# A separate prologue for two batches in a fused attention and routed feed-forward kernel

## The chip, the cores and the metric

The kernel runs on one core of a Trainium2 chip. The metric is the device time in microseconds; each kernel is run several times and the median is compared. The profile is of one execution.

## What is computed

Eight batches of 256 rows of 256 values pass through one layer: x plus cross attention of its layer norm over a context (16 heads of 16, a strictly lower triangular mask, softmax), and then plus a feed-forward of eight experts of which each row takes two, within a capacity. Cut to what matters:

```python
qh = (layernorm(x) @ W_q).reshape(B, S, 16, 16)
kh = (ctx @ W_k).reshape(B, S, 16, 16)
vh = (ctx @ W_v + b_v).reshape(B, S, 16, 16)
scores = einsum('bihd,bjhd->bhij', qh, kh) / 4
probs  = softmax(where((j < i) | (i == 0) & (j == 0), scores, -inf))
x = x + einsum('bhij,bjhd->bihd', probs, vh).reshape(B, S, 256) @ W_o + b_o
x = x + routed_ffn(layernorm(x), wg, w1, b1, w2, b2)   # top 2 of 8
```

All of it is float32; the kernel splits operands into high and low parts to get there with faster matmuls.

## The kernel before

The program has two parts, attention() and experts(). The change is in attention() alone. There every engine has an order written out by hand: its function defines small pieces (queries, keys, a_scores, exp, maxima, split_queries, mask and so on) and a step(s) that calls them, and steps() runs step(s) for s from -2 to 8. One step works on up to four batches at once: it projects batch s+2 (proj_part), finds the maxima of batch s+1 (max_part), computes the probabilities and the values of batch s (score_part) and writes out batch s-1 (out_part). Engines meet only at semaphores, which each piece waits for and counts up.

For one batch the pieces follow one another so:

- Projection. SyncE loads the context into c_sb and ScalarE rounds it to cT_hi (round_context), GpSimd takes the rest, cT_lo (split_context). VectorE gathers the statistics of x (norm_stats, next_stats), GpSimd makes the scale and shift (powers, norm_powers), ScalarE normalises (norm_x), TensorE transposes (turn_x, line L808), ScalarE rounds to xT_hi (L401), VectorE takes the rest, xT_lo (L566). Then queries and keys (project_turned, twelve matmuls each, L851) go to bank[1] and bank[0] in PSUM. Of each result ScalarE takes q_h or k_h (L401), VectorE the rest (q_rest, k_rest, L574), GpSimd the middle and low parts (split_rest, L263 and L265), and SyncE stacks the parts by DMA into Qs and Ks (stack, L202), three transfers of the high part, two of the middle and one of the low for each.
- Maxima. a_scores computes twelve units of scores (L752) with a mask (L755), VectorE reduces each to its maximum (maxima, L596); a unit may begin when the reduction two units back is done. split_maxima, turn_maxima (L840) and copy_maxima (L472) bring the maxima into two rows of Qs by a DMA on ScalarE's queue (L474).
- Probabilities and values. b_scores (L766, L769) in four groups of four heads, exp (L423), mask on GpSimd (L323 to L325), values (L785, L786), with V from project_values (L862) and add_value_bias (L613).
- Output. turn_values (L801), normalise, turn_attention, outputs, add_output, the second layer norm and the router.

The weights are split once: round_weights on ScalarE (L398), split_weights on VectorE (L561). project_values writes bank[0], which the keys of the same step use too, so it waits for k_rest and, the first times, for all four weights:

```python
            def project_values(s):
                if first(s, 1):
                    pe.wait_ge(k_rest_ready, s + 2)
                    pe.wait_ge(w_lo_ready, 4)
                project(bank[0], 2, cT_hi, cT_lo, v_done)
```

Steps -2 and -1 are the prologue. Step -2 projects batch 0. Step -1 on TensorE is project_values (batch 0), turn_x (batch 1), all twelve units of maxima of batch 0, turn_maxima, and then queries and keys of batch 1. Step 0 is of the general form, with queries and keys of batch 2 in it.

Of the kernel before, what the change touches and what calls it, by code (L numbers as in the profile page):

```python
# [6 lines left out]
P = 128  # L7
# [9 lines left out]
HEADS = 16  # L17
# [26 lines left out]
def attention(nc, sem, sb, persist, x, ctx_in, Wq, Wk, Wv, bv, Wo, bo, wg, w1, b1, w2, b2, xn_rows, out):  # L44
# [20 lines left out]
    bank = [ps[:, 2, :], ps[:, 6, :]]  # L65

# [10 lines left out]
    c_sb = sb("c_sb", [P, 2, S], F32)  # L77
    xn = sb("xn", [P, 2, D], F32)
    st1 = sb("st1", [P, 2, 6], F32)
    mv1 = sb("mv1", [P, 2, 2], F32)  # L80
    ve1 = sb("ve1", [P, 2, 2], F32)
    rs1 = sb("rs1", [P, 2, 2], F32)
# [31 lines left out]
    x0_loaded, x_loaded = sem("x0_loaded"), sem("x_loaded")  # L114
    ctx_loaded = sem("ctx_loaded")
# [33 lines left out]
    def steps(step):  # L149

        for s in range(-2, B + 1):
            step(s)
# [22 lines left out]

    def first(s, n):

        return s < n
# [6 lines left out]
    with block:  # L185

        @block.sync
        def _(sp):
            sp.dma_start(x_all[:, 0:2, :], x_tiles[:, 0:2, :]).then_inc(x0_loaded, 16)
            sp.dma_start(c_sb[:, :, :], ctx_tiles[0]).then_inc(ctx_loaded, 16)  # L190
            sp.dma_start(w_raw[:, 0], Wq.rearrange("(k p) n -> p k n", p=P)).then_inc(wqkvo_loaded[0], 16)
            sp.dma_start(w_raw[:, 1], Wk.rearrange("(k p) n -> p k n", p=P)).then_inc(wqkvo_loaded[1], 16)
            sp.dma_start(w_raw[:, 2], Wv.rearrange("(k p) n -> p k n", p=P)).then_inc(wqkvo_loaded[2], 16)
            sp.dma_start(w_raw[:, 3], Wo.rearrange("(k p) n -> p k n", p=P)).then_inc(wqkvo_loaded[3], 16)
            sp.dma_start(x_all[:, 2:, :], x_tiles[:, 2:, :]).then_inc(x_loaded, 16)
# [9 lines left out]
            def step(s):  # L205
                to = (s + 2) % BUFS
                if proj_part(s) and s + 3 < B:
                    sp.wait_ge(cT_lo_ready, s + 3)
                    sp.dma_start(c_sb[:, :, :], ctx_tiles[s + 3]).then_inc(ctx_loaded, 16)
                if proj_part(s):  # L210
# [11 lines left out]
                    sp.wait_ge(k_h_ready, s + 3)  # L222
                    stack(Ks[to], K_PARTS, "h", k_part["h"], k_stacked)
# [8 lines left out]

            steps(step)
# [4 lines left out]
        def _(pool):  # L238
            pool.dma_start(bv_bc[:, :], bv.rearrange("(a n) -> a n", a=1).broadcast_to([P, D])).then_inc(small_loaded, 16)
            pool.dma_start(bo_bc[:, :], bo.rearrange("(a n) -> a n", a=1).broadcast_to([P, D])).then_inc(small_loaded, 16)  # L240
# [100 lines left out]
            def step(s):  # L341
# [19 lines left out]
                if s == -1:  # L361
                    norm_powers(2)
# [1104 lines left out]
```

## Time and profile before

| | us |
|---|---|
| median of 3 runs | 475.74 (475.26 to 476.03) |
| the profiled execution | 474.79 |
| its span | 473.0 |
| TensorE busy in the span | 378.9 (80%) |
| VectorE busy | 294.4 (62%) |
| GpSimd busy | 227.1 (48%) |
| ScalarE busy | 188.2 (40%) |
| granted TensorE clock, mean | 0.908 |

Attention takes about the first 225 us of the span and the experts the rest. A busy share says how long an engine worked, not what it was waited for; a timeline's row shows the idle time before it in brackets and what ended it. The granted clock is 1.00 at 2.4 GHz and 0.50 at 1.2 GHz.

### The profile page before, as it was taken

To read this page: it belongs to the slowest core of one execution; us is meant where nothing else is said; L and a number is where in the kernel's file an instruction comes from. 1 tells how busy PE (TensorE), PEld (TensorE's weight loads), DVE (VectorE), ACT (ScalarE), POOL (GpSimd) and SP (SyncE) were. 2 spreads that over 40 slices of the span, in tenths; PEclk is the share of its full clock that TensorE was granted. 3 is DMA by queue.
4 is the path that set the end of the run, shared out by engine and by line. 5 is a ranking of instruction groups with operands and counts; after the bars stand their busy time and mean duration, and the time that the engine had idled before them with its cause. 6 is when DMAs were issued, how large, how long until landed. Compare 5 with 4: busy or idle time off the path is not lost. (4 is left out here: it accounts for less than half of the span.)

```text
span 473.0 us, 8086 instructions
## 1 busy us (share of the span) xinstructions
PE 378.9 (80%) x3005; PEld 320.8 (68%) x3026; DVE 294.4 (62%) x614; ACT 188.2 (40%) x255; POOL 227.1 (48%) x311
## 2 busy tenths in 40 slices
PE   0566589999989898976422689999999999999970
PEld 0545467777768686664311479898989898999960
DVE  3445366776777666742269676868676777777540
ACT  3212345655555563634112252526262626262210
POOL 5773964756666662523114840717171717150504
PEclk9858799999999999988555599999999999999995
DMA  7621463606152528122110610818181818140303
GB/s 220 202 67 36 122 178 72 178 28 177 47 158 60 145 54 228 46 92 95 57 39 11 245 56 2 230 49 232 47 239 37 242 37 246 34 52 1 45 1 44
DMA packets 35735, 49.10 MB, mean 104 GB/s; under 512 B 4734, under 2 KB 31536, under 8 KB 34672
## 3 DMA queue, kind: packets, MB, share of 16 engines
q1 hardware_dynamic: 27744, 35.42, 24.7%
q0 software_dynamic: 6272, 8.57, 9.8%
q10 hardware_dynamic: 1680, 4.60, 3.0%
q8 instruction: 24, 0.39, 0.4%
q14 instruction: 15, 0.12, 0.1%
HBM read 27.57 MB, written 8.39 MB: 76 GB/s over the span
## 5 line engine op out<-in xcount | busy, mean ns | idle before, releaser
L1146 POOL DMA_INDIRECT out_dram<-Y,scatter_idx x32 | 52.0, 1624 | 109.0 <-DVE Y L1297 101.7
L1188 ACT ACTIVATE hr<-ps,b_sb 128x512 f32<-128x512 f32 x64 | 43.4, 688 | 109.0 <-PE ps L1356 72.0
L1366 PE MATMUL ps<-w_hi,h_hi 128*128 128x256 f32 x256 | 72.9, 285 | 1.6 <-DVE h_lo L1279 1.6
L1366 PE MATMUL ps<-w_lo,h_hi 128*128 128x256 f32 x256 | 72.4, 283 | 0.0
L1366 PE MATMUL ps<-w_hi,h_lo 128*128 128x256 f32 x256 | 72.4, 283 | 0.0
L596 DVE TENSOR_REDUCE nm<-ps 128x2 f32<-128x512 f32 (+1 forms) x96 | 61.8, 683 | 15.8 <-PE ps L755 9.0
L423 ACT ACTIVATE PT<-ps 128x1536 f32<-128x1536 f32 x32 | 46.4, 1451 | 26.4 <-PE ps L769 25.5
L1277 DVE CAST h_hi<-hr 128x512 fp32r<-128x512 f32 x64 | 29.1, 455 | 43.3 <-ACT hr L1188 43.1
L1356 PE MATMUL ps<-XT_hi,w_hi 128*128 128x512 f32 x128 | 51.3, 400 | 1.5 <-DVE XT_lo L1266 1.5
L1366 PEld LDWEIGHTS ps<-w_hi,h_hi 128*128 128x128 f32 x256 | 48.9, 191 | 3.8 <-DVE h_lo L1279 2.1
L1356 PE MATMUL ps<-XT_hi,w_lo 128*128 128x512 f32 x128 | 51.1, 399 | 0.0
L1356 PE MATMUL ps<-XT_lo,w_hi 128*128 128x512 f32 x128 | 50.5, 394 | 0.0
L1366 PEld LDWEIGHTS ps<-w_hi,h_lo 128*128 128x128 f32 x256 | 49.0, 191 | 1.6
L1366 PEld LDWEIGHTS ps<-w_lo,h_hi 128*128 128x128 f32 x256 | 49.0, 191 | 0.0
L752 PE MATMUL ps<-Ks,Qs 126*128 126x256 bf16 (+1 forms) x256 | 38.7, 259 | 9.1 <-issue 4.6
L1279 DVE TENSOR_TENSOR h_lo<-hr,h_hi 128x512 fp32r<-128x512 f32 x64 | 44.6, 697 | 2.2
L1133 POOL DMA_INDIRECT Xg<-xn_rows,gather_idx x32 | 35.1, 1098 | 16.1 <-issue 9.6
L752 PEld LDWEIGHTS ps<-Ks,Qs 126*128 126x128 bf16 x256 | 19.3, 101 | 19.8 <-DVE nm L596 10.2
L1356 PEld LDWEIGHTS ps<-XT_hi,w_hi 128*128 128x128 f32 x128 | 24.8, 193 | 5.6 <-issue 1.9
L1356 PEld LDWEIGHTS ps<-XT_lo,w_hi 128*128 128x128 f32 x128 | 24.5, 191 | 5.5
L1356 PEld LDWEIGHTS ps<-XT_hi,w_lo 128*128 128x128 f32 x128 | 24.7, 193 | 3.3
L785 PE MATMUL ps<-PT,V 128*32 128x256 f32 x256 | 21.1, 391 | 4.2 <-POOL PT L325 4.2
(174 smaller groups left out, 832.4 us busy)
## 6 DMA issues: line engine op xcount, KB each, us to landing
raw<-in_L_ffn_w_dram SPq DMA_DIRECT2D x12, 1024.0 KB, 7.4
raw<-in_L_ffn_w_dram ACTq DMA_DIRECT2D x4, 1024.0 KB, 5.6
Qs<-q_h SPq DMA_DIRECT2D x24, 128.0 KB, 2.4
Ks<-k_h SPq DMA_DIRECT2D x24, 128.0 KB, 2.5
c_sb<-in_ctx_dram SPq DMA_DIRECT2D x8, 256.0 KB, 2.8
Qs<-q_m SPq DMA_DIRECT2D x16, 128.0 KB, 2.5
Ks<-k_m SPq DMA_DIRECT2D x16, 128.0 KB, 2.5
xn_rows<-x2n SPq DMA_DIRECT2D x8, 256.0 KB, 2.5
```

Of the source, the lines that this page charges most:

```text
L423: act.activation(PT[g % 2][:, :], prob_score, ACT.Exp, scale=float(HD) ** -0.5).then_inc(exp_done, 1)
L596: dve.tensor_reduce(nm[:, tile, h:h + count], max_bank[u % 2].rearrange("p (h j) -> p h j", h=count), AX_X, ALU.max, negate=True).then_inc ...
L752: pe.matmul(max_bank[u % 2][:, h * width:(h + 1) * width], Q[0:ROWS, h0 + h, tile * P:(tile + 1) * P], K[0:ROWS, h0 + h, 0:width], start=( ...
L785: pe.matmul(out, V[s % 2][:, 0, h, :], PT[g % 2][:, hh * S:(hh + 1) * S], start=True, stop=False)
L1133: pool.indirect_dma_start(Xg[q][:, j, :], None, xn_rows[:, :], bass.IndirectOffsetOnAxis(ap=gather_idx[q][:, j:j + 1], axis=0)).then_inc(g ...
L1146: pool.indirect_dma_start(out_rows[:, :], bass.IndirectOffsetOnAxis(ap=scatter_idx[q][:, j:j + 1], axis=0), Y[q][:, j, :], None, bounds_ch ...
L1188: act.activation(hr[c % 2][:, :], h_bank[c % 4], ACT.Relu, bias=b1_sb[q][:, c:c + 1]).then_inc(hr_ready, 1)
L1277: dve.tensor_copy(h_hi[c % 4][:, :], hr[c % 2][:, :]).then_inc(hh_ready, 1)
L1279: dve.tensor_tensor(h_lo[c % 4][:, :], hr[c % 2][:, :], h_hi[c % 4][:, :].bitcast(F32), ALU.subtract).then_inc(hl_ready, 1)
L1356: last = pe.matmul(h_bank[c % 4], w[q][:, k, c, :], a[q][:, k, :], start=(n == 1), stop=(n == 6))
L1366: last = pe.matmul(y_bank[j // 2][:, (j % 2) * D:(j % 2 + 1) * D], a[c % 4][:, j * P:(j + 1) * P], w[q][:, c, :], start=(c == 0 and n == 0 ...
```

## The change

It takes steps -2 and -1 out of the common loop and writes them out on each engine as a prologue of its own:

- TensorE projects batch 0, then the values of batch 0, then batch 1, and only then runs the maxima of batch 0. The first projections use three PSUM banks of their own (first_bank, part of what the probabilities use later). Step 0 has an order of its own: maxima of batch 1, queries, keys, b_scores and values interleaved anew, turn_maxima before the last two value groups.
- The context has two buffers (c_sb[0], c_sb[1], loaded two batches ahead) and so have the statistics and powers of the first layer norm (st1, mv1, ve1, rs1), so that batch 1's need not wait for batch 0's normalisation.
- Wq and Wk are loaded from ScalarE's queue; biases and router weights from SyncE's instead of GpSimd's; batch 1's x by itself; Wo and the rest of x only after Wv has landed.
- The three stacks of the first keys' high part are issued by ScalarE (stack_first_keys).
- Wo's low part is made by VectorE behind the maxima of batch 0, and TensorE waits for it in step 1, at outputs. GpSimd fills the key buffers and makes its constants in another order; add_bias of the first two batches comes last.

Left out of the diff are the renamings that follow from the doubled buffers, the removal of the old prologue's cases from each step(), and waits that count the same things in the new order.

```diff
+    first_bank = [ps[:, 3, :], ps[:, 4, :], ps[:, 5, :]]
...
+    def query_bank(s):
+
+        return first_bank[0] if s == -2 else bank[1]
+
+    def key_bank(s):
+
+        return first_bank[1] if s == -2 else bank[0]
+
+    def values_bank(s):
+
+        return first_bank[2] if s == -1 else bank[0]
...
+            def load_context(n):
+                sp.dma_start(c_sb[n % 2][:, :, :], ctx_tiles[n]).then_inc(ctx_loaded[n % 2], 16)
+
             sp.dma_start(x_all[:, 0:2, :], x_tiles[:, 0:2, :]).then_inc(x0_loaded, 16)
-            sp.dma_start(c_sb[:, :, :], ctx_tiles[0]).then_inc(ctx_loaded, 16)
-            sp.dma_start(w_raw[:, 0], Wq.rearrange("(k p) n -> p k n", p=P)).then_inc(wqkvo_loaded[0], 16)
-            sp.dma_start(w_raw[:, 1], Wk.rearrange("(k p) n -> p k n", p=P)).then_inc(wqkvo_loaded[1], 16)
+            load_context(0)
+            sp.dma_start(x_all[:, 2:4, :], x_tiles[:, 2:4, :]).then_inc(x1_loaded, 16)
             sp.dma_start(w_raw[:, 2], Wv.rearrange("(k p) n -> p k n", p=P)).then_inc(wqkvo_loaded[2], 16)
+            load_context(1)
+            sp.dma_start(bv_bc[:, :], bv.rearrange("(a n) -> a n", a=1).broadcast_to([P, D])).then_inc(small_loaded, 16)
+            sp.dma_start(bo_bc[:, :], bo.rearrange("(a n) -> a n", a=1).broadcast_to([P, D])).then_inc(small_loaded, 16)
+            sp.dma_start(wg_sb[:, :, :], wg.rearrange("(k p) e -> p k e", p=P)).then_inc(small_loaded, 16)
+            sp.wait_ge(wqkvo_loaded[2], 16)
             sp.dma_start(w_raw[:, 3], Wo.rearrange("(k p) n -> p k n", p=P)).then_inc(wqkvo_loaded[3], 16)
-            sp.dma_start(x_all[:, 2:, :], x_tiles[:, 2:, :]).then_inc(x_loaded, 16)
+            sp.dma_start(x_all[:, 4:, :], x_tiles[:, 4:, :]).then_inc(x_loaded, 16)
...
-                if proj_part(s) and s + 3 < B:
+                if s + 4 < B:
                     sp.wait_ge(cT_lo_ready, s + 3)
-                    sp.dma_start(c_sb[:, :, :], ctx_tiles[s + 3]).then_inc(ctx_loaded, 16)
+                    load_context(s + 4)
...
-                    sp.wait_ge(k_h_ready, s + 3)
-                    stack(Ks[to], K_PARTS, "h", k_part["h"], k_stacked)
+                    if s > -2:
+                        sp.wait_ge(k_h_ready, s + 3)
+                        stack(Ks[to], K_PARTS, "h", k_part["h"], k_stacked)
...
+            step(-2)
+            step(-1)
             steps(step)
...
-            pool.dma_start(bv_bc[:, :], bv.rearrange("(a n) -> a n", a=1).broadcast_to([P, D])).then_inc(small_loaded, 16)
-            pool.dma_start(bo_bc[:, :], bo.rearrange("(a n) -> a n", a=1).broadcast_to([P, D])).then_inc(small_loaded, 16)
-            pool.dma_start(wg_sb[:, :, :], wg.rearrange("(k p) e -> p k e", p=P)).then_inc(small_loaded, 16)
...
+            mask_constants()
+            norm_powers(0)
+            split_context(-2)
+            norm_powers(1)
+            fill_keys(0)
+            buffer_constants(0)
+            fill_keys(1)
+            split_queries(-2)
+            split_keys(-2)
+            split_context(-1)
+            split_queries(-1)
+            split_keys(-1)
+            norm_powers(2)
+            fill_keys(2)
+            zero_queries(2)
+            buffer_constants(1)
+            add_bias(0)
+            add_bias(1)
+            routing_constants()
             steps(step)
...
         def _(act):
+            act.dma_start(w_raw[:, 0], Wq.rearrange("(k p) n -> p k n", p=P)).then_inc(wqkvo_loaded[0], 16)
+            act.dma_start(w_raw[:, 1], Wk.rearrange("(k p) n -> p k n", p=P)).then_inc(wqkvo_loaded[1], 16)
...
+            def stack_first_keys():
+                wait_alone(act, started, k_filled[0], 1)
+                wait_alone(act, started, k_h_ready, 1)
+                for part, c in enumerate(K_PARTS):
+                    if c == "h":
+                        act.dma_start(Ks[0][part::PARTS, :, :].rearrange("d (h f) t -> d h (f t)", f=2),
+                                      k_part["h"][:, :, :].rearrange("p f t -> p (f t)")).then_inc(k_stacked, 16)
...
-                    if score_part(s):
+                    if s == 0:
+                        round_queries(s)
+                        exp(s, 0)
+                        round_keys(s)
+                        exp(s, 1)
+                    elif score_part(s):
                         exp(s, 0)
                         exp(s, 1)
-                    if first(s, -1):
...
-                    if proj_part(s):
+                    if proj_part(s) and s > 0:
                         round_queries(s)
...
             round_weights(0)
+            round_context(-2)
+            round_weights(1)
             norm_x(0)
-            round_weights(1)
+            round_x(-2)
+            norm_x(1)
+            round_queries(-2)
+            round_weights(2)
+            round_keys(-2)
+            stack_first_keys()
+            round_x(-1)
+            round_context(-1)
+            round_weights(3)
+            round_queries(-1)
+            round_keys(-1)
+            norm_x(2)
+            copy_maxima(-1)
             steps(step)
 
...
             def next_stats(s):
-                if first(s, -1):
+                if s == -2:
+                    dve.wait_ge(x1_loaded, 16)
+                if s == -1:
                     dve.wait_ge(x_loaded, 16)
-                dve.wait_ge(xn_ready, 2 * (s + 3))
-                norm_stats(x_all[:, bass.ds(2 * (s + 3), 2), :], st1, mv1, ln1_stats, s + 3)
+                if s > -2:
+                    dve.wait_ge(xn_ready, 2 * (s + 2))
...
+            dve.wait_ge(x0_loaded, 16)
+            norm_stats(x_all[:, 0:2, :], st1[0], mv1[0], ln1_stats, 0)
+            split_weights(0)
+            next_stats(-2)
+            split_weights(1)
+            split_x(-2)
+            dve.memset(Qs[1][:, :, :].rearrange("p h t -> p (h t)").bitcast(F32), 0.0).then_inc(q_zeroed[1], 1)
+            split_queries(-2)
+            split_weights(2)
+            split_keys(-2)
+            split_x(-1)
+            add_value_bias(-1)
+            split_queries(-1)
+            split_keys(-1)
+            next_stats(-1)
+            for pair in range(UNITS // 2):
+                maxima(-1, pair)
+            split_maxima(-1)
+            split_weights(3)
+            dve.memset(x2n[:, :, :], 0.0).then_inc(x2n_stored, 16)
             steps(step)
             dve.wait_ge(top_used, 3 * B)
...
+                    if s == 0:
+                        pe.wait_ge(v_ready, 1)
...
             def outputs(s):
                 pe.wait_ge(aT_lo_ready, s)
+                if s == 1:
+                    pe.wait_ge(w_lo_ready, 4)
...
-                if s == -1:
+                if s == 0:
                     project_values(s)
                     turn_x(s)
                     a_scores(s, 0)
-                    for pair in range(1, UNITS // 2):
-                        a_scores(s, pair)
+                    a_scores(s, 1)
+                    queries(s)
+                    a_scores(s, 2)
+                    b_scores(s, 0)
+                    keys(s)
+                    a_scores(s, 3)
+                    b_scores(s, 1)
+                    a_scores(s, 4)
+                    values(s, 0)
+                    b_scores(s, 2)
+                    a_scores(s, 5)
+                    values(s, 1)
+                    b_scores(s, 3)
                     turn_maxima(s)
-                    queries(s)
-                    keys(s)
+                    values(s, 2)
+                    values(s, 3)
                 elif B - 3 < s < B:
...
+            turn_x(-2)
+            queries(-2)
+            keys(-2)
+            project_values(-1)
+            turn_x(-1)
+            queries(-1)
+            keys(-1)
+            for pair in range(UNITS // 2):
+                a_scores(-1, pair)
+            turn_maxima(-1)
             steps(step)
```

On ScalarE, from the program's start to the rounding of the first queries. Before (w_hi are the rounded weights, by what they wait for; xn is the normalised x, xT_hi and cT_hi the rounded x and context, q_h the high part of the queries):

```order
L398 ACT_TABLE_LOAD
L398 ACTIVATE w_hi<-w_raw 128x512 [waits wq_loaded]
L407 ACTIVATE xn<-x_all,rs 128x256 [waits ln1_pow,started]
L407 ACTIVATE xn<-x_all,rs 128x256
L398 ACTIVATE w_hi<-w_raw 128x512 [waits wk_loaded]
L401 ACTIVATE cT_hi<-c_sb 128x512 [waits ctx_loaded]
L401 ACTIVATE xT_hi<-ps 128x512 [waits tx_done]
L398 ACTIVATE w_hi<-w_raw 128x512 [waits wv_loaded]
L401 ACTIVATE q_h<-ps 128x512 [waits q_done]
```

and in the change:

```order
L407 DMA w_raw<-in_L_xattn_W_q_dram 128x2x256
L408 DMA w_raw<-in_L_xattn_W_k_dram 128x2x256
L422 ACT_TABLE_LOAD
L422 ACTIVATE w_hi<-w_raw 128x512 [waits wq_loaded]
L425 ACTIVATE cT_hi<-c_sb 128x512 [waits ctx_loaded0]
L422 ACTIVATE w_hi<-w_raw 128x512 [waits wk_loaded]
L431 ACTIVATE xn<-x_all,rs_0 128x256 [waits ln1_pow,started]
L431 ACTIVATE xn<-x_all,rs_0 128x256
L425 ACTIVATE xT_hi<-ps 128x512 [waits tx_done]
L431 ACTIVATE xn<-x_all,rs_1 128x256 [waits started,tx_done,ln1_pow]
L431 ACTIVATE xn<-x_all,rs_1 128x256
L425 ACTIVATE q_h<-ps 128x512 [waits q_done]
```

The context's rounding and that of Wk have moved ahead of the normalisation, and batch 1's normalisation ahead of the first queries.

On ScalarE in step 0, up to the third exponential (PT are the probabilities, of b_scores). Before:

```order
L401 ACTIVATE cT_hi<-c_sb 128x512 [waits v_done,ctx_loaded]
L401 ACTIVATE xT_hi<-ps 128x512 [waits q_done,tx_done]
L423 ACTIVATE PT<-ps 128x1536 [waits b_done] x2
L401 ACTIVATE q_h<-ps 128x512 [waits q_stacked,q_done]
L401 ACTIVATE k_h<-ps 128x512 [waits k_stacked,k_done]
L423 ACTIVATE PT<-ps 128x1536 [waits av_done,b_done]
```

and in the change:

```order
L425 ACTIVATE cT_hi<-c_sb 128x512 [waits v_done,ctx_loaded0]
L425 ACTIVATE xT_hi<-ps 128x512 [waits q_done,tx_done]
L425 ACTIVATE q_h<-ps 128x512 [waits q_stacked,q_done]
L455 ACTIVATE PT<-ps 128x1536 [waits b_done]
L425 ACTIVATE k_h<-ps 128x512 [waits k_stacked,k_done]
L455 ACTIVATE PT<-ps 128x1536 [waits b_done]
L455 ACTIVATE PT<-ps 128x1536 [waits av_done,b_done]
```

The roundings of the queries and of the keys have moved ahead of the first and the second exponential.

## Rows read from the trace of the kernel before

**Rows 1.** Busy time by stretches, all engines; start:end, length, busy us (instructions), clock, DMA

```profile
48.00:60.00 12.00, 7.23 (x54) 5.83 (x58) 4.05 (x6) 4.20 (x5) 10.67 (x21) 0.72 0.40 110
```

**Rows 2.** Timeline of TensorE; start us, us, operation, count [idle before <- releaser]

```profile
13.47 0.58 PE L851 MATMUL ps<-xT_hi,w_hi 128*128 128x256 f32 x1 [1.91 <-DVE xT_lo L566]
...
22.34 0.55 PE L862 MATMUL ps<-w_hi,cT_hi 128*128 128x256 f32 x1 [3.96 <-DVE w_lo L561]
...
53.97 0.59 PE L752 MATMUL ps<-Ks,Qs 126*128 126x256 bf16 x2 [4.35 <-issue]
...
70.12 0.66 PE L785 MATMUL ps<-PT,V 128*32 128x256 f32 x8 [0.98 <-POOL PT L325]
...
71.00 0.39 PE L862 MATMUL ps<-w_hi,cT_hi 128*128 128x256 f32 x1
...
74.58 0.61 PE L766 MATMUL ps<-Qs,Ks 128*128 128x256 bf16 x4 [0.43 <-DMA Qs<-nmT]
```

**Rows 3.** Timeline of VectorE, the additions of V's bias in steps 1 and 2

```profile
72.74 0.69 DVE L613 TENSOR_TENSOR V<-ps,bv_bc 128x512 f32<-128x512 f32 x1 [2.05 <-PE ps L862]
...
95.51 0.69 DVE L613 TENSOR_TENSOR V<-ps,bv_bc 128x512 f32<-128x512 f32 x1 [2.00 <-PE ps L862]
```

**Rows 4.** Timeline of SyncE's queue, the last stack of batch 1's keys

```profile
51.46 0.60 SPq L202 DMA_DIRECT2D Ks<-k_l  x1
```

**Rows 5.** DMA issues of the first 60 us; KB each, median us to landing

```profile
x_all<-in_x_dram SPq DMA_DIRECT2D x1, 1792.0 KB, 13.6
...
Ks<-k_m SPq DMA_DIRECT2D x4, 128.0 KB, 2.4
...
w_raw<-in_L_xattn_W_k_dram SPq DMA_DIRECT2D x1, 256.0 KB, 8.7
```

**Rows 6.** Timeline of ScalarE

```profile
9.31 1.08 ACT L407 ACTIVATE xn<-x_all,rs 128x256 f32<-128x256 f32 x2
...
16.43 0.60 ACT L401 ACTIVATE q_h<-ps 128x512 bf16<-128x512 f32 x1 [3.22 <-PE ps L851]
...
40.33 1.25 ACTq L474 DMA_DIRECT2D Qs<-nmT  x1
...
56.73 1.45 ACT L423 ACTIVATE PT<-ps 128x1536 f32<-128x1536 f32 x1 [5.13 <-PE ps L769]
```

**Rows 7.** Timeline of GpSimd

```profile
5.07 0.24 POOL L300 TENSOR_SCALAR ve<-mv 128x2 f32<-128x2 f32 x1 [1.04 <-DVE mv L556]
...
6.77 1.80 POOL L253 MEMSET Ks<- 128x2048 f32 x1
...
58.30 0.20 POOL L323 TENSOR_SCALAR_AFFINE_SELECT PT<-PT 128x4 f32<-128x4 f32 x1 [1.06 <-ACT PT L423]
...
61.20 0.61 POOL L263 CAST q_m<-q_rest 128x512 bf16<-128x512 f32 x1 [1.47 <-DVE q_rest L574]
...
63.63 0.61 POOL L263 CAST k_m<-k_rest 128x512 bf16<-128x512 f32 x1 [0.57 <-DVE k_rest L574]
```

**Rows 8.** TensorE alone by stretches of 1 us; length, busy us (instructions), clock, DMA

```profile
20.00:21.00 1.00, 0.00 (x0) 0.97 0.76 212
...
34.00:35.00 1.00, 0.91 (x4) 0.71 0.07 24
...
41.00:42.00 1.00, 1.00 (x8) 0.71 0.09 25
...
44.00:45.00 1.00, 1.00 (x5) 0.59 0.00 0
...
51.00:52.00 1.00, 0.00 (x0) 0.83 0.76 207
```

**Rows 9.** Timeline of VectorE, the reductions of batch 0's maxima

```profile
30.10 1.28 DVE L596 TENSOR_REDUCE nm<-ps 128x2 f32<-128x512 f32 x2
...
34.37 4.68 DVE L596 TENSOR_REDUCE nm<-ps 128x4 f32<-128x512 f32 x7 [0.16 <-PE ps L755]
```

More of the change, by code:

```diff
@@ L76, in attention @@
     half = sb("half", [P, 2], F32)
-    c_sb = sb("c_sb", [P, 2, S], F32)
+    c_sb = [sb(f"c_sb{q}", [P, 2, S], F32) for q in range(2)]
     xn = sb("xn", [P, 2, D], F32)
[L79 to L82, printed above, removed]
+    st1 = [sb(f"st1_{q}", [P, 2, 6], F32) for q in range(2)]
+    mv1 = [sb(f"mv1_{q}", [P, 2, 2], F32) for q in range(2)]
+    ve1 = [sb(f"ve1_{q}", [P, 2, 2], F32) for q in range(2)]
+    rs1 = [sb(f"rs1_{q}", [P, 2, 2], F32) for q in range(2)]
     st2 = sb("st2", [P, 2, 6], F32)
@@ L111, in attention @@
     idx8 = sb("idx8", [P, 2, 8], U32)
-    x0_loaded, x_loaded = sem("x0_loaded"), sem("x_loaded")
-    ctx_loaded = sem("ctx_loaded")
+    x0_loaded, x1_loaded, x_loaded = sem("x0_loaded"), sem("x1_loaded"), sem("x_loaded")
+    ctx_loaded = [sem(f"ctx_loaded{q}") for q in range(2)]
     wqkvo_loaded = [sem(f"w{n}_loaded") for n in "qkvo"]
@@ L149, in steps @@
     def steps(step):
-        for s in range(-2, B + 1):
+        for s in range(B + 1):
             step(s)
@@ L360, in step @@
                     mask(s, 1)
-                if s == -1:
-                    norm_powers(2)
-                if proj_part(s) and s > -2:
+                if proj_part(s):
                     split_queries(s)
@@ L711, in step @@
                         maxima(s, 1)
-                    if first(s, -1):
-                        split_weights(2)
                     if proj_part(s):
                         split_queries(s)
-                    if proj_part(s) and not first(s, -1) and not (s + 3 >= B):
+                    if s + 3 < B:
                         next_stats(s)
@@ L867, in queries @@
                 pe.wait_ge(xT_lo_ready, s + 3)
-                if first(s, -1):
+                if s == -2:
                     pe.wait_ge(w_lo_ready, 1)
@@ L871, in queries @@
                     pe.wait_ge(x2_ready, s)
-                elif first(s, 0):
-                    pe.wait_ge(nmT_ready, s + 2)
-                else:
-                    pe.wait_ge(q_rest_ready, s + 2)
-                project_turned(bank[1], 0, xT_hi, xT_lo, q_done)
+                elif s == 0:
+                    pe.wait_ge(nmT_ready, 1)
+                project_turned(query_bank(s), 0, xT_hi, xT_lo, q_done)
             def keys(s):
@@ L912, in step @@
                     a_scores(s, 0)
-                    for pair in range(1, UNITS // 2):
-                        a_scores(s, pair)
+                    a_scores(s, 1)
[11 more added lines that the diff above has]
+                    b_scores(s, 3)
                     turn_maxima(s)
-                    queries(s)
-                    keys(s)
+                    values(s, 2)
+                    values(s, 3)
                 elif B - 3 < s < B:
```

97 lines of the change are left out of this document (27 added, 70 removed).

## The prediction

> **What bounds the kernel now.** I read the busy time by stretches first. Between 48 and 60 us TensorE is busy 7.23 of 12 us, at a mean granted clock of 0.72 [rows 1]: the expensive part of the span is its beginning. Then TensorE's timeline up to the second step. Its first projection starts at 13.47; the maxima scores of batch 1 start at 53.97 after 4.35 us without a matmul; the last value group of step 0 starts at 70.12 and step 1 at 71.00 [rows 2]. From there a step lasts 22.77 us (the two V additions at 72.74 and 95.51 [rows 3]), whatever the prologue did. So I price only one thing: how much earlier step 1 starts. Everything behind it (six more steps, then the experts, which stand as one TensorE chain) has the same order in both kernels and should move along.
>
> What the 4.35 us wait for is on SyncE's queue: the last stack of batch 1's keys is issued at 51.46 [rows 4] and such a transfer lands 2.4 us after its issue [rows 5], so at 53.9. It is late because batch 1's projections come behind batch 0's twelve maxima.
>
> **The change, place by place.** All times are from the span's start, by the durations of the one profiled execution.
>
> *Weights and the first rows.* Today Wk lands 8.7 us after its issue, so at 11.0, and ScalarE normalises batch 0 at 9.31 [rows 5, 6]. The new order on ScalarE is Wq, context, Wk, then batch 0; so Wk's landing counts twice as much as before. Bounds: a 128 KB transfer alone lands in 2.4 us, giving about 4; as now, 11.0 [rows 5]. Issued together now are six pieces of 256 KB, the 1792 KB block of x [rows 5] and 264 KB of biases and router weights, 3592 KB; of these the block will wait for Wv, and seven pieces and the 264 KB remain, 2056 KB. Scaling 8.7 by 2056/3592 gives 5.0, at an issue of about 1.3 some 6.3. I take 7.0, since two queues share the engines. GpSimd's powers of batch 0 run from 5.07 to 6.8 [rows 7]; they now stand behind the mask constants, which begin at once, since GpSimd's three DMA issues go to SyncE. I take them to be done when the statistics are, and the powers to end near 7.1. ScalarE: Wk's rounding to 7.7, batch 0 to 8.8. Now the start of the normalisation at 9.31 is followed by the first projection matmul 4.16 later [rows 2, 6]; two activations that stood in between go ahead of it, worth 0.5. First projection at 7.7 + 3.7 = 11.4, **2.1 us earlier**.
>
> *To the end of batch 1's projections.* Queries and keys take 5.0 together (cold at first: one projection takes 2.96 from its first matmul to the start of its reader, 13.47 to 16.43, against 1.74 warm, 71.00 to 72.74 [rows 2, 3, 6]), so k_h starts at 16.3. The values of batch 0 and the turn of batch 1 run to 18.3. On ScalarE the three added issues follow k_h: 3 x 0.63, at most 3 x 1.25 (the one issue there now took 1.25 [rows 6]); to 18.8, so they delay batch 1's xT_hi by only 0.5. What is queued behind them: xT_hi (0.60), then VectorE's xT_lo (0.69 [rows 3, 6]), and the queries at 20.2. TensorE has then been idle for 1.9 us. The clock fell to 0.5 at 20.9 and 51.7 after pauses; between them it fell at 41.4 and came back 3.4 us later [rows 8]. I take the middle one: both projections take 4.7 (warm 3.3), to 24.9. Stacks: GpSimd has filled both key buffers by 14.5 (the powers of two batches, one context split, two fills of 1.80 [rows 7] and V's constants), SyncE issues the last stack of batch 0 at 19.9, landed at 22.4, ahead of the keys' end. The three issues taken from SyncE would have made that 24.8, so moving them buys nothing unless the clock stays up.
>
> *Maxima of batch 0.* k_h and k_rest to 26.3, the statistics (0.9) to 27.2, twelve reductions at 0.67 (seven in 4.68 [rows 9]) to 35.3. Their transpose, copy and transfer: nmT issued at 36.6. The later issue of the large block of x costs nothing: issued at 9 to 10, it needs no more than the 13.6 us it takes now [rows 5], and the statistics that want it stand at 26.3. Wo's low part runs behind the maxima and is needed only in step 1: nothing.
>
> *Step 0.* Values projection from 36.1, V at 38.4, the turn to 39.0: batch 1's maxima scores start at 39.0 instead of 53.97, **15 us earlier**. The stacks of batch 1 (last landing near 31) are 8 us early: the stall is gone. But step 0's new order gives half of it back. The first exponential now stands behind four units of maxima, the queries and a third pair: b_scores(0,0) ends at 45.35. exp(0,0) to 46.8, then k_h to 47.4, k_rest to 48.1, two reductions to 49.4, the seventh and eighth units to 49.8, b_scores(0,1) to 50.65, exp(0,1) to 52.1. Today it ends at 56.73 + 1.45 = 58.18 [rows 6]: **6.1 us earlier**. That is the number that counts, since from here GpSimd sets the end: from 58.30 to the mask that releases values(0,3) at 70.12 it works in one piece but for two waits of 1.47 and 0.57 for q_rest and k_rest [rows 2, 7]. Those waits go, because both are there at 48.1: 9.8 us of work, so the last mask at 61.9 and values(0,3) **8.2 us earlier**.
>
> *What is late next.* TensorE then has little to do between 55 and 62 (about 2 us of value groups and maxima's transpose), and I expect the clock to have fallen when step 1 begins, as at 51.7 [rows 8]. One projection cold is 1.22 more; the last value group, two turns and a b_scores group add 0.7: **+1.9**. The wait of 0.43 for nmT at step 1 [rows 2] goes, since the maxima are transposed before the last two value groups: **-0.4**.
>
> Context double buffering and the second statistics home change nothing later: neither is waited for in the steady step. Sum: -8.2 + 1.9 - 0.4 = **-6.7 us**. The profiled execution took 474.79 (span 473.0), 0.95 under the median of 475.74; from the median the sum gives **469.1**.
>
> The clock rows say that a fall can cost more than its pause: after 3.96 us without a matmul before 22.34 [rows 2] the clock fell at 20.9 and was back only at 34.4 [rows 8]. The Trainium skill (TensorE: Matmul & The Clock Gate, HAM oscillation) has the same warning in general form: bursts of matmuls with pauses between them restart at the lower clock. [...]
>
> **Rivals.**
> *The weights land as late as now.* If the second queue brings no bandwidth of its own and Wk still lands at 11.0, batch 0 is normalised at 11.7 instead of 7.7, all behind it 4 us later: 473.1. For it: at 8.7 us Wk took more than three times as long as a transfer of half its size does alone [rows 5], so it is sharing that sets it. Against: 43% of the bytes are held back. The Trainium skill (DMA: Bandwidth & Descriptors, Issuing engines are not separate DMA queues) says that transfers issued from several engines share the same DMA engines and only issue time is saved, which speaks for this one. Chance 0.15.
> *The clock stays up.* No fall at 21 and none before step 1: 1.4 (4.7 to 3.3) and 1.9 less, 465.8. Chance 0.10.
> *The step gives back more.* If the new order of step 0 leaves values(0,2) and (0,3) to wait for GpSimd and step 1 inherits the delay (late OT copies, late xn of batch 3), I price one mask group and one powers group, 3.2: 472.3. Chance 0.10.
> *Slower.* The clock does not come back between 21 and 50, because the new prologue has many short pauses: reductions then follow at 0.85 (five in 4.27, from 30.10 to 34.37 [rows 9]) instead of 0.67, +2.2; four more cold projections, +4.9; four score groups and two turns on the chain, +1.7; 8.8 in all: 477.9. It decides once the clock is low for more than three quarters of that stretch. For it: 13.5 us at 0.5 in the present prologue [rows 8]. Against: there TensorE was mostly idle. Chance 0.05. That the stall stays as it is, with an unchanged time, has 0.03: only if batch 1's stacks landed 8 us later than computed.
>
> **How the numbers follow.** Forecast 0.57, the faster rivals 0.35, slower 0.05, no change 0.03. A measurement of this kernel tells about 0.2% (1 us) from no change; all cases but the last two lie beyond it: faster 0.92, same 0.03, slower 0.05. The range goes from the warm case with Wk at the scaled 6.3 (465.8 less 0.7) to the late weights (473.1) with 0.9 on top for the execution-to-execution place of the clock's falls: 465.0 to 474.0.
>
> **What would show it.** Right: first L895 matmul near 11.4; no idle time over 1 us before the first maxima scores of batch 1, which start near 39; exp(0,1) ending near 52; GpSimd busy without a wait from there to the last mask near 62; step 1 near 63 to 64. Wrong: Wk landing after 9 (late weights); a granted clock of 1.00 at 21 to 25 and at 58 to 66 (warm case); stretches 24 to 48 mostly at 0.5 (slower); TensorE waiting for q_stacked or k_stacked.

## The result and the profile after

The change takes 472.87 us (470.52 to 474.92, 12 runs), beside 475.42 for the kernel before in the same sets of runs: the ratio is 0.9947 with a 95% interval of 0.9932 to 0.9962, so some 2.5 us faster. The forecast was 6.7. The profiled execution took 472.27 with a span of 470.5; against the one of before (474.79, 473.0) that is 2.5 as well, so the two traces can be laid side by side. One execution of e8, further down, ran slow (479.73 us at a mean clock of 0.81, the others at 0.93), and its median leaves it out. Warm below means a granted clock of 1.00, cold 0.50.

TensorE's timeline; the rows answer to [rows 2]:

```profile
11.32 0.58 PE L895 MATMUL ps<-xT_hi,w_hi 128*128 128x256 f32 x1 [1.41 <-DVE xT_lo L606]
...
20.65 0.38 PE L895 MATMUL ps<-xT_hi,w_hi 128*128 128x256 f32 x1 [2.26 <-DVE xT_lo L606]
...
37.38 0.40 PE L884 MATMUL ps<-identb,nm_s 128*32 128x128 bf16 x2 [2.12 <-DVE nm_s L687]
...
42.39 0.64 PE L794 MATMUL ps<-Ks,Qs 126*128 126x256 bf16 x2
...
54.44 0.39 PE L794 MATMUL ps<-Ks,Qs 126*128 126x256 bf16 x2 [2.01 <-DVE nm L636]
...
67.45 1.11 PE L829 MATMUL ps<-PT,V 128*32 128x256 f32 x8 [1.67 <-POOL PT L345]
```

The first projection starts at 11.32 (13.47 before, 11.4 forecast), and batch 1's maxima scores at 42.39, without idle time, instead of 53.97 behind 4.35 us. The stall is gone. The pause of 2.26 us ahead of 20.65 is the one after which the forecast had the clock fall (it stayed at 1.00 there), that of 2.01 ahead of 54.44 belongs to the new order: batch 1's seventh unit waits for a reduction that stands behind k_rest on VectorE. But the maxima scores were forecast for 39.0, and from there the kernel falls behind the working, by 3.4 us here and by 5.6 at exp(0,1). VectorE's V additions of steps 1 and 2, as in [rows 3], and the reductions and nm_s before them:

```profile
27.15 3.37 DVE L636 TENSOR_REDUCE nm<-ps 128x2 f32<-128x512 f32 x5
...
36.02 1.07 DVE L685 CAST nm_s<-nm 128x32 bf16<-128x32 f32 x1
37.13 0.19 DVE L687 TENSOR_TENSOR nm_s<-nm,nm_s 128x32 bf16<-128x32 f32 x1
...
71.38 0.69 DVE L653 TENSOR_TENSOR V<-ps,bv_bc 128x512 f32<-128x512 f32 x1 [9.74 <-PE ps L906]
...
93.89 0.69 DVE L653 TENSOR_TENSOR V<-ps,bv_bc 128x512 f32<-128x512 f32 x1 [2.00 <-PE ps L906]
```

Step 1 comes only 1.36 us earlier (72.74 before) and is itself 0.26 shorter, 22.51. At the last V addition the lead is 1.9 (185.77 before, 183.89 now), and the last 0.6 comes between there and the experts, where the trace of before has 3.4 us at 0.50 (from 205 us on) and this one has none. The experts take 232 us in every run of this document. TensorE alone by stretches of 1 us; the last three numbers are the granted clock, the DMA share and GB/s, as in [rows 8]:

```profile
29.00:30.00 1.00, 0.66 (x5) 0.81 0.78 202
...
36.00:37.00 1.00, 0.00 (x0) 0.72 0.00 0
...
49.00:50.00 1.00, 1.00 (x8) 0.50 0.00 0
...
50.00:51.00 1.00, 1.00 (x11) 0.95 0.19 41
...
63.00:64.00 1.00, 0.00 (x0) 0.87 1.11 296
...
70.00:71.00 1.00, 1.00 (x8) 0.71 0.03 8
```

The clock is at its lower level (0.50, 1.2 GHz) from 29.6 to 33.0, from 36.4 to 50.1 and from 63.7 to 70.6. The last fall was in the forecast; the first two were not. The long one covers the values projection of batch 1, half its maxima scores and the queries of batch 2; the keys of batch 2 start at 50.77, warm. Together the three make 23.9 us, and the trace of before has 23.9 too (13.6, 3.4 and 6.8): the change does not lose more to the clock than the old kernel, but the working had left most of it out. Ahead of 16 us the column can't be used: it shows 1.00 while the projections' matmuls start 0.21 us apart, as in the cold stretches, and 0.12 apart from 16.1 on. ScalarE's timeline, as [rows 6]:

```profile
7.65 1.09 ACT L431 ACTIVATE xn<-x_all,rs 128x256 f32<-128x256 f32 x2 [0.85 <-POOL rs L325]
...
17.23 1.94 ACTq L439 DMA_DIRECT2D Ks<-k_h  x3
...
23.09 0.60 ACT L425 ACTIVATE q_h<-ps 128x512 bf16<-128x512 f32 x1 [2.18 <-DMA Qs<-q_l]
24.90 0.60 ACT L425 ACTIVATE k_h<-ps 128x512 bf16<-128x512 f32 x1 [1.22 <-DMA Ks<-k_l]
...
56.24 1.45 ACT L455 ACTIVATE PT<-ps 128x1536 f32<-128x1536 f32 x1 [3.18 <-PE ps L813]
```

exp(0,1) ends at 57.69 (58.18 before, 52.1 forecast): nearly the whole 11.6 us by which batch 1's maxima scores start earlier is gone by here. DMA issues of the first 60 us, as in [rows 5]:

```profile
x_all<-in_x_dram SPq DMA_DIRECT2D x1, 1536.0 KB, 9.2
...
Ks<-k_m SPq DMA_DIRECT2D x4, 128.0 KB, 4.0
Ks<-k_h ACTq DMA_DIRECT2D x3, 128.0 KB, 4.3
...
w_raw<-in_L_xattn_W_k_dram ACTq DMA_DIRECT2D x1, 256.0 KB, 4.7
```

Wk lands 4.7 us after its issue at 1.30, at 6.0, against 8.7 and a landing at 11.0. So the weights were no brake.

### The profile page after: what moved, and what is told of

It reads as the page before. It is cut to its first block and busy times, and to the rows that moved or that the text cites. A ratio compares the mean times of both kernels' runs of the same rounds, so it can differ in the third digit from the quotient of the medians.

```text
span 470.5 us, 8109 instructions
## 1 busy us (share of the span) xinstructions
PE 381.5 (81%) x3026; PEld 320.6 (68%) x3026; DVE 297.4 (63%) x615; ACT 188.6 (40%) x255; POOL 224.4 (48%) x307
## 5 line engine op out<-in xcount | busy, mean ns | idle before, releaser
L1199 POOL DMA_INDIRECT Xg<-xn_rows,gather_idx x32 | 35.6, 1112 | 16.1 <-issue 9.6
L797 PE MATMUL ps<-mask,identb 128*128 128x256 bf16 (+1 forms) x96 | 31.5, 328 | 0.0
L343 POOL TENSOR_SCALAR_AFFINE_SELECT PT<-PT 128x4 f32<-128x4 f32 x32 | 6.5, 204 | 46.1 <-ACT PT L455 46.0
```

The source lines that it names most:

```text
L343: pool.affine_select(p0[:, :, 0:1], p0[:, :, 0:1], [[0, HPG], [0, 1]], ALU.is_ge, 0.0, base=0, channel_multiplier=-1)
L797: pe.matmul(diag, identb[:, :], mask1[:, :, :] if tile else mask0[:, :, :], start=False, stop=True, skip_group_check=True).then_inc(a_done, 1)
L1199: pool.indirect_dma_start(Xg[q][:, j, :], None, xn_rows[:, :], bass.IndirectOffsetOnAxis(ap=gather_idx[q][:, j:j + 1], axis=0)).then_inc(g ...
```

## The experiments

Four theories on the missing 4 us. **A**: the low clock in step 0. **B**: the new order of step 0, whatever the clock. **C**: VectorE's cast of 1.07 us (0.18 before) beside a pass of GpSimd. **D**: the moved stacks. All times are medians with the ratio to the kernel before in the same set of runs (474.9 to 475.5 there). Each trace is of one execution, and executions of one kernel differ in where the clock falls.

**e1_warm_step0.** The clock held by matmuls without a result, in waits of TensorE; nothing else changes.

```diff
+            def warm(bank_, count):
+                for _ in range(count):
+                    pe.matmul(bank_, identb[:, :], mask0[:, :, :].rearrange("p a b -> p (a b)"), start=True, stop=True)
...
                     project_values(s)
+                    warm(value_bank, 3)
                     turn_x(s)
                     a_scores(s, 0)
+                    warm(value_bank, 3)
                     a_scores(s, 1)
...
                     keys(s)
+                    warm(value_bank, 7)
                     a_scores(s, 3)
...
+            a_scores(-1, 0)
+            warm(value_bank, 5)
+            for pair in range(1, UNITS // 2):
                 a_scores(-1, pair)
+            warm(value_bank, 7)
             turn_maxima(-1)
```

> The changed kernel plus 25 matmuls without a result (128x512 bf16, written to PSUM banks nobody reads then): 5 after the first two units of batch 0's maxima, 7 before turn_maxima(-1), 3 before turn_x(0), 3 after the first pair of batch 1's maxima, 7 before its seventh unit. They fill waits of TensorE. Theory A, the low clock from 36.3 to 50.0 us is what the prediction lacked: it stays at 1.00 there, exp(0,1) ends near 53 instead of 57.7, the whole takes 4 to 5 us less than the changed kernel (about 468.5). Rival B, the new order of step 0 itself is what gives the gain back, whatever the clock: exp(0,1) stays near 57, the whole within 1 us of the changed kernel.

Measured: 468.46 us (0.9858, 0.9827 to 0.9888), 4.4 less than the change. TensorE by stretches, and ScalarE's exp(0,1), of this run:

```profile
30.00:36.00 6.00, 4.74 (x29) 1.00 0.31 83
36.00:50.00 14.00, 12.17 (x89) 1.00 0.18 49
...
60.00:66.00 6.00, 3.93 (x27) 0.50 0.44 95
```

```profile
50.86 1.45 ACT L455 ACTIVATE PT<-ps 128x1536 f32<-128x1536 f32 x1 [3.18 <-PE ps L813]
```

The clock stays at 1.00 through step 0, and exp(0,1) ends at 52.31, where the forecast had 52.1. More work on TensorE made the kernel 4.4 us shorter (4.2 by the ratios). Theory A stands: with the clock held the forecast's time is reached. In the traces 0.56 of the 5.4 us at exp(0,1) stand ahead of the first added matmul (k_h of batch 1 at 24.34 for 24.90), so they are not the work of the added matmuls.

**e2_general_step0.** Step 0 in the general order; the new prologue stays.

```diff
-                if s == 0:
-                    project_values(s)
...
-                elif B - 3 < s < B:
+                if B - 3 < s < B:
...
-                    if s == 0:
-                        round_queries(s)
-                        exp(s, 0)
-                        round_keys(s)
-                        exp(s, 1)
-                    elif score_part(s):
+                    if score_part(s):
```

> The changed kernel with step 0 in the general order on TensorE and ScalarE (b_scores(0,0) first, both exponentials before the queries' rounding); prologue as changed. Rival B: exp(0,1) ends 8 us or more earlier, the last mask 5 to 6 us earlier, about 467. Theory A alone: the order costs nothing, because the queries and keys end later by what the exponentials gain; within 1 us of the changed kernel (472 to 474).

Measured: 462.80 us (0.9732, 0.9698 to 0.9766), 10 us less than the change and 4 below what rival B had expected. Its ScalarE and VectorE:

```profile
45.54 1.45 ACT L455 ACTIVATE PT<-ps 128x1536 f32<-128x1536 f32 x1 [0.93 <-PE ps L808]
```

```profile
60.57 0.69 DVE L648 TENSOR_TENSOR V<-ps,bv_bc 128x512 f32<-128x512 f32 x1 [1.98 <-PE ps L901]
```

exp(0,1) ends at 46.99 and V of step 1 stands at 60.57, 10.8 earlier. Its granted clock from 36 on is 1.00 (6.8 us at 0.50 lie ahead, from 27 to 34), so this run alone mixes A and B; e5 and e8 separate them.

**e3_bias_early.** GpSimd's pass over x ahead of its fills.

```diff
             norm_powers(2)
+            add_bias(0)
+            add_bias(1)
             fill_keys(2)
...
             buffer_constants(1)
-            add_bias(0)
-            add_bias(1)
             routing_constants()
```

> The changed kernel with GpSimd's two add_bias passes moved ahead of its fills, so that they do not run while VectorE makes nm_s. Theory C, VectorE's cast at 36.02 took 1.07 instead of 0.18 us because GpSimd's pass over x ran beside it: the cast takes 0.18 again, 0.9 us less in all (472.0). Rival: the cast was long for another reason; no change.

Measured: 470.22 us (0.9895, 0.9870 to 0.9921), 2.6 less where C allowed 0.9. The cast takes 0.47 instead of 1.07, and the clock stays at 1.00 between 36 and 50 in this run, with no matmul added:

```profile
36.14 0.47 DVE L685 CAST nm_s<-nm 128x32 bf16<-128x32 f32 x1
```

```profile
36.05 0.52 POOL L268 MEMSET V<- 128x512 f32 x1
```

```profile
36.00:50.00 14.00, 8.66 (x74) 1.00 0.18 49
```

The profile is of the fastest of the six executions (468.71; their mean clocks run from 0.911 to 0.918), so it shows more of the clock's part than the median has. TensorE's pause ahead of turn_maxima is 1.52 us here and 2.12 in the change, but that the shorter cast kept the clock up is not shown; e4 speaks against it. C and A were mixed again, hence e10.

**e4_keys_sync.** The stacks of the first keys back on SyncE's queue.

```diff
-                    if s > -2:
-                        sp.wait_ge(k_h_ready, s + 3)
-                        stack(Ks[to], K_PARTS, "h", k_part["h"], k_stacked)
+                    sp.wait_ge(k_h_ready, s + 3)
+                    stack(Ks[to], K_PARTS, "h", k_part["h"], k_stacked)
...
-            stack_first_keys()
```

> The changed kernel with the three stacks of the first keys' high part back on SyncE's queue, in the old place. The prediction's view: they were moved for nothing, the last stack lands at 24.8 and nobody waits, ScalarE is free 1.9 us earlier: within 0.5 us or up to 0.5 faster. Rival D: batch 1's rounding already waits for these stacks now (0.75 us for the queries', 1.1 us for the keys'), so a later last stack is paid in full: 1 to 2 us slower (474 to 475).

Measured: 470.39 us (0.9896, 0.9869 to 0.9924): 2.5 less than the change, where D expected more time and the prediction's view at most 0.5 less. TensorE's turn_maxima, and its clock:

```profile
36.96 0.28 PE L882 MATMUL ps<-identb,nm_s 128*32 128x128 bf16 x2 [2.14 <-DVE nm_s L685]
```

```profile
36.00:37.00 1.00, 0.04 (x1) 1.00 0.00 0
42.00:43.00 1.00, 0.61 (x4) 0.62 0.73 185
36.00:50.00 14.00, 9.74 (x71) 0.88 0.18 47
```

Its clock between 36 and 50 was 0.88, against 0.52, so the price of the stacks can't be read here; e7 repeats it with the clock held. The cast took 1.10 us here and the pause ahead of turn_maxima was 2.14, as long as in the change, yet the clock was 1.00 in it and fell only at 42.2, for 3.4 us. The pause alone doesn't decide the fall.

**e5_warm_all.** e1 with fourteen more such matmuls, in the waits ahead of step 1.

```diff
                     turn_maxima(s)
+                    warm(max_bank[0], 8)
                     values(s, 2)
+                    warm(max_bank[0], 6)
                     values(s, 3)
```

> e1_warm_step0 plus 8 matmuls without a result after turn_maxima(0) and 6 before values(0,3), into a bank whose maxima are done. Theory A: the clock no longer falls at 60 us, step 1 begins warm; the last mask to V of step 1 takes 3.3 us (as in e2_general_step0) instead of 4.9: 1.5 to 2 us under e1_warm_step0, about 466.7. Rival: TensorE's work there is hidden, no change from 468.5.

Measured: 467.41 us (0.9822, 0.9792 to 0.9852), 1.05 less than e1 by the medians of two sets of runs, whose intervals overlap. The profile is clearer; VectorE's V of step 1 and TensorE by stretches:

```profile
64.72 0.69 DVE L653 TENSOR_TENSOR V<-ps,bv_bc 128x512 f32<-128x512 f32 x1 [8.32 <-PE ps L906]
```

```profile
60.00:66.00 6.00, 4.74 (x42) 1.00 0.50 103
```

V of step 1 stands at 64.72, in e1 at 66.50; the last masks end at 62.16 and 62.02. From mask to V it is 2.56 warm and 4.48 cold: 1.9 us, the size that the forecast gave this fall. In the change it is 3.98 (67.40 to 71.38), since the clock came back at 70.6: 1.4.

**e6_before_warm.** The kernel before, with matmuls without a result in the waits of its prologue. It answers what the change is worth with the clock taken out on both sides.

```diff
                 project_turned(bank[0], 1, cT_hi, cT_lo, k_done)
+                if first(s, -1):
+                    for _ in range(28):
+                        pe.matmul(value_bank[:, 0:S], w_hi[:, 0, 0, 0:P], xT_hi[:, 0, :], start=True, stop=True)
...
                     project_values(s)
+                    pe.wait_ge(const_ready, 4)
+                    warm(value_bank, 9)
                     turn_x(s)
...
+                    warm(value_bank, 5)
                     turn_maxima(s)
                     queries(s)
                     keys(s)
+                    warm(value_bank, 4)
...
                         turn_x(s)
+                    if s == 0:
+                        warm(value_bank, 17)
```

> The kernel before with matmuls without a result in its prologue's waits of TensorE (28 of 256 columns after the first keys, 9 before turn_x(-1), 5 before turn_maxima(-1), 4 before the values of step 0, 17 before batch 1's maxima). Theory A: the clock stays at 1.00 from 18 to 70 us; the old order has cold work too (maxima, queries and keys of batch 1, the first half of step 0), so it gains 3 to 4 us, about 471.5; its warm form is then some 5 us slower than the warm form of the change, which is what the change is worth with the clock taken out. Rival: the old order gains nothing, since its waits are for DMA, GpSimd and VectorE (474.5 to 475).

Measured: 471.98 us (0.9924, 0.9897 to 0.9951): the old order loses 3.5 us to the clock too, less than the 4.4 to 5.5 of the change (e1, e5). Its clock was not quite held (0.84 from 30 to 36, 0.95 to 50: 3.4 us at 0.50). Against e5, 467.41 in the same runs, the change is worth 4.6 with nearly all of the clock taken out on both sides.

**e7_warm_all_keys_sync.** e5 with e4's edit.

> e5_warm_all with the three stacks of the first keys' high part back on SyncE's queue. With the clock held, this is the price of the moved stacks alone. The prediction's view (moved for nothing): within 0.5 us of e5_warm_all. Rival D (the last stack's landing is waited for): 1 to 2 us slower. Rival E (the three issues hold ScalarE before xT_hi, and moving them back helps): 0.5 to 1.5 us faster.

Measured: 467.80 us (0.9845, 0.9816 to 0.9874), e5 467.41. Its ScalarE:

```profile
21.42 0.60 ACT L424 ACTIVATE q_h<-ps 128x512 bf16<-128x512 f32 x1 [1.46 <-PE ps L893]
24.50 0.60 ACT L424 ACTIVATE k_h<-ps 128x512 bf16<-128x512 f32 x1 [2.49 <-DMA Ks<-k_l]
```

V of step 1 stands at 64.63 (e5: 64.72). With the stacks on one queue batch 1's queries are rounded at once and the keys wait until 24.50; with two queues both wait (22.57 and 24.62 in e5; 23.09 and 24.90 in the change). With two queues the pieces issued up to 20 us land 3.3 to 4.7 us after issue (medians by piece, in the change), on one queue 2.4 to 2.6 (here), the load of x being under way at first in both. (On the one queue the pieces of batch 1's queries, issued from 23.4 on, take 3.4 to 3.6.) Moving them bought nothing that these runs can tell (0.4 us, where each interval reaches 1.4 either way), as forecast, though for a reason it did not give.

**e8_general_bias_warm.** e2 with e3's edit and the prologue's twelve matmuls of e1.

> e2_general_step0 with add_bias early and with the 12 matmuls without a result in the prologue only (5 after the first pair of batch 0's maxima, 7 before turn_maxima(-1)). Theories A and C: the prologue stays warm, the cast takes 0.18; 1 to 1.5 us under e2_general_step0, about 461.5. Rival: the general order hides both, 462.8.

Measured: 460.69 us (0.9688, 0.9659 to 0.9717), 2.1 below e2 where 1 to 1.5 were expected. The cast took 0.71 beside a memset, not 0.18, and the clock was at 0.50 for 3.4 us from 26.8, so the prologue was not held warm throughout. V of step 1 at 60.23:

```profile
60.23 0.69 DVE L648 TENSOR_TENSOR V<-ps,bv_bc 128x512 f32<-128x512 f32 x1 [1.99 <-PE ps L901]
```

Beside e5 in the same runs, both at 1.00 from 36 us on: 4.5 us earlier by this row, 6.7 by the medians. But e8 enters step 0 later: V of step 0 stands at 39.73, in e5 at 38.28. From V of step 0 to V of step 1 it is 20.50 against 26.44, and the same two numbers come back within 0.03 in e9 and e2, and in e7 and e10. That is theory B with the clock held: the new order of step 0 costs 5.9 us. From the transposes of turn_maxima to b_scores(0,0) it takes 8.5 us (36.37 to 44.89 in e5), in the general order 3.2 (37.78 to 41.02 in e8). What these two profiles differ in behind the last V addition (57.2 us to the experts' first instruction in e5, 54.1 in e8) is not the order's: e7, with e5's order, has 55.5 there, and e9, with e8's, 56.5.

**e9_general_warm_keys_sync.** e8 with e4's edit: the fastest version.

> e8_general_bias_warm with the three first stacks on SyncE's queue again. After e7 (no difference with the clock held) the moved stacks should be worth nothing here too: within 1 us of e8_general_bias_warm's 460.8. Rival: without the stall of the late exponentials batch 1's stacks count again, and the time rises by 1 us or more.

Measured: 460.30 us (0.9679, 0.9658 to 0.9700): 15 us under the kernel before, and the same as e8, as expected.

**e10_warm_all_bias_early.** e5 with e3's edit.

> e5_warm_all with add_bias early. Theory C with the clock held: VectorE's two small instructions that make nm_s took 0.18 + 1.14 us in e5 beside GpSimd's pass over x; beside its fills they take 0.5 to 0.7 together, so the maxima's transpose comes 0.6 us earlier and step 1 too: V of step 1 near 64.1 (64.72 in e5), 466.8. The rest of e3's gain (2.6 us) was then the clock. Rival: the 2.6 us come from GpSimd's order itself and show here as well (465).

Measured: 468.80 us (0.9855, 0.9828 to 0.9881), where 466.8 was expected. nm_s and GpSimd beside it:

```profile
36.75 1.22 DVE L685 CAST nm_s<-nm 128x32 bf16<-128x32 f32 x1
38.01 0.19 DVE L687 TENSOR_TENSOR nm_s<-nm,nm_s 128x32 bf16<-128x32 f32 x1
```

```profile
35.68 1.80 POOL L276 MEMSET Qs<- 128x2048 f32 x1
37.42 0.53 POOL L268 MEMSET V<- 128x512 f32 x1
```

The cast ends at 37.97, when GpSimd's second memset ends (37.95). So C was half wrong: a fill holds VectorE's cast as well as the pass over x does, and the place of add_bias settles nothing. In the change, too, the cast outlasts the pass (over at 36.53) and ends at 37.09, with a memset of GpSimd's constants (37.06). What e3 gained beyond that was the clock, as far as the runs tell. In this run batch 0's last query stack also landed 2 us later than in e5 (q_h of batch 1 at 24.71 for 22.57), TensorE stood still for 2.6 us and the clock was at 0.50 for 3.4 us from 25.8. The delay is there at nm_s (36.75 for 34.97), which accounts for V of step 1 at 66.60: from nm_s to V the two runs agree within 0.1.

**e11_change_again.** The change, unaltered.

> The changed kernel, unaltered, on the chip of this call, to have its time beside the others: 472.9 within 1 us. Theory A: where its profile shows a later or shorter fall of the clock between 36 and 50 us, V of step 1 comes earlier than 71.38 by about half the cold time saved.

Measured: 472.37 us (469.72 to 475.68, 11 runs; 0.9938, 0.9911 to 0.9965). V of step 1 at 71.90, and its clock:

```profile
36.00:50.00 14.00, 9.90 (x61) 0.76 0.06 20
```

The expected link of the two did not show, since this run was already 1.8 us late at nm_s (37.81) and cold at 30 to 36 (0.59). It shows when all the cold time up to 72 us is added up (from the stretches of 1 us, from 16 on) and set beside V of step 1, for the executions with the change's step 0:

| | us at 0.50 up to 72 | V of step 1 |
|---|---|---|
| the change | 23.9 | 71.38 |
| e11 | 23.9 | 71.90 |
| e4 | 17.1 | 68.91 |
| e3 | 10.3 | 66.97 |
| e1 | 6.8 | 66.50 |
| e10 (late stack) | 3.4 | 66.60 |
| e5 | 0 | 64.72 |
| e7 | 0 | 64.63 |

Within one kernel the time goes with the clock as well: of the change's twelve executions the fastest (470.52) had a mean clock of 0.915, the slowest (474.92) 0.898. The spread is no sign of its own: the change's runs reach over 4.4 and 6.0 us in the two sets, the kernel before over 1.7 in the one and 3.7 in the other.

## Why the prediction was wrong

- *What bounds the kernel, and that only step 1's start counts*: right in the main. From the second step on the steps last 22.5 us in all of these kernels (22.7 now and then), and the experts 232. But of the 2.5 us measured only 1.4 stand at step 1; without the 1.1 behind it the forecast would have missed by more.
- *Weights and first rows*, 2.1 us earlier: 2.15, with luck in it. Wk at 6.0 lies by the scaled 6.3, 1 us ahead of the 7.0 that was taken; the rival of late weights is out. The step's real bound was GpSimd's powers, ending at 7.55 for 7.1 (xn at 7.65 waits for them).
- *Queries and keys of batch 1 at 4.7 because of a fall at 21*: the end was right by luck (k_h at 24.90 for 24.9), the cause wrong. The clock stayed at 1.00. The queries started 0.45 late (20.65), as ScalarE's three issues held xT_hi for 0.9 us and not 0.5, and of the 4.25 us from there 0.75 and 1.15 were waits for stacks. The last of these landed 4.6 us after issue, not 2.4, beside ScalarE's stacks (e7); the 2.4 came from stacks alone on one queue.
- *Maxima of batch 0 to 35.3*: the last reduction ends at 35.99; the clock was low from 29.6 to 33.0, and with it held they take 8.05 us for the forecast's 8.1 (e1).
- ***Step 0* is the step that failed.** It was summed with warm durations throughout, with the argument's only fall put behind it. The runs showed a clock at 0.50 from 36.4 to 50.1, which is the whole way from turn_maxima to b_scores(0,0). A second, smaller term was mis-sized: from the last reduction to turn_maxima the working left some 0.5 us; it was 1.4 (35.99 to 37.38), 0.9 of it the cast held by GpSimd, and TensorE's own pause was 2.1 (35.26 to 37.38). At exp(0,1) the change is 5.6 us behind the forecast; holding the clock gives 5.4 of it back in the trace and 4.4 in the median (e1). With the clock held the step's own numbers come out: exp(0,1) at 52.31 for 52.1, the last mask at 62.02 for 61.9, 468.5 us for 469.1. Two errors cancel in that: the reductions end 0.7 early in e1 (34.64 for 35.3), and nm_s takes 1.5 us (34.67 to 36.15) in place of about 0.4.

  | us | forecast | the change | e1 |
  |---|---|---|---|
  | last reduction of batch 0 ends | 35.3 | 35.99 | 34.64 |
  | values projection starts | 36.1 | 37.70 | 36.41 |
  | maxima scores of batch 1 start | 39.0 | 42.39 | 39.44 |
  | b_scores(0,0) ends | 45.35 | 50.96 | 45.58 |
  | exp(0,1) ends | 52.1 | 57.69 | 52.31 |
  | last mask ends | 61.9 | 67.40 | 62.02 |

  Why the clock fell at 36.4 is open: the pause in front of it was 2.1 us, and e4 had the same pause and no fall in it.
- *GpSimd as the bound from exp(0,1) to the last mask*, 9.8 us: right, 9.7 (57.69 to 67.40).
- *+1.9 for a cold start of step 1*: right in kind and by the pair of e5 and e1 (1.9); in the change's own trace it is 1.4.
- *The rivals*: "slower" had the right mechanism and put 8.8 us on it; the clock was low for 17 of the 29 us named (21 to 50), and 4.4 came of it. The sign given for it came true (15 of the 24 us from 24 to 48 at 0.50) while the kernel was still faster: it had been priced as all or nothing, with a chance of 0.05 and no case for a part of it.
- *That step 0's order gives half of the lead back* was in the working, and e2 and e8 show it: 5.9 us from V to V with the clock held, 10 as it stands. The order puts b_scores(0,0) behind six units of maxima and the queries; in the general order it runs as soon as nmT has landed.
- *A slip of reading*: 34.4 for the clock's return in the trace of before is 34.6 by its own row (0.71 from 34 to 35), so that stretch is 13.6 us and not 13.5. Nothing hangs on it.

## What to carry to other kernels

When an order is changed, list TensorE's new pauses and price the stretch behind each of them at both clock levels; here that difference was over 4 of the 7 us forecast. Which pause brings a fall could not be told from its length: 2.1 us did in one trace and not in another. Where a gain seems lost, put matmuls without a result into the waits: if the kernel gets shorter, the clock had it, and the rest of the comparison can be made with the clock held on both sides. Don't read an edit's price from a pair of kernels whose clocks differ: e3 and e4 each took 2.5 us less than the change, and with the clock held or nearly held nothing of that was left (e10 and e7 beside e5).

## What the runs showed of the hardware

- VectorE's cast of 128x32 elements, 0.18 us alone, took 1.07 in the change, 0.47 in e3 and 1.22 in e10, ending within 0.04 us of the end of a GpSimd memset each time (in the change it began beside the pass over x). In e5 it took 0.18 at 34.97, where one of the pass's two instructions gave way to the next. The two-operand instruction behind it stayed at 0.19 beside the memsets of e3 and e10, but took 1.14 in e5 (35.18 to 36.32), until GpSimd's pass over x (33.76 to 36.26) was done. The Trainium skill (SBUF — State Buffer, SBUF: two separate sides) tells the two apart in the same way: the port pair that both engines use goes to whoever starts first, for its whole instruction; a cast in a two-port mode competes with any GpSimd instruction, an instruction with two SBUF inputs only with one that reads SBUF. The rows agree with that; whether this cast runs in such a mode no row shows.
- In the change the clock fell 1.2 us into the pause of 2.1 us (granted clock 1.00 before) and was at 1.2 GHz for 13.7 us although TensorE was busy in most of them ([rows 8] have a stretch of the same length); it did not fall in e3 after a pause of 1.52, nor in e4 in one of 2.14, where it fell 5 us later and for 3.4 us. The pauses of 2.26 us before 20.65 and of 2.01 before 54.44 had no such fall behind them either. What decides when it falls and when it comes back is not settled here.
- 128 KB transfers within the core's memory issued up to 20 us landed 2.4 to 2.6 us after issue from one queue (e7), and 3.3 to 4.7 with a second queue issuing the same kind beside it (the change). Later ones in e7, issued from one queue in one long row and beside a load of context, took up to 3.6.
